# A finished batch's chain over 150 ticks instead of 126, its last steps one iteration later, with semaphores of their own and two other PSUM banks

## The chip, the core and the metric

The kernel runs on one core of one Trainium2 chip. The metric is the device time of one execution in microseconds (us). A core has five engines that run programs of their own and meet through semaphores: TensorE (PE; its weight loads are listed as PEld), VectorE (DVE), ScalarE (ACT), GpSimd (POOL) and SyncE (SP, which here only issues DMAs).

## What is computed

One perceiver block on 16 batches of 128 tokens with 512 numbers each. Cross attention to a context of 2048 rows (16 heads, one shared key and value head), then a linear attention with decay over chunks of 64 tokens (4 heads; a triangular system is solved for each), then a router that sends each token to one of 16 experts, of which each takes the first 128.

```
x = x + xattn(layernorm(x), ctx)            # softmax(Q K^T) V Wo + bo
x = x + retention(layernorm(x))             # (eye - A0)^-1 per chunk, then @ Wr
x = x + ffn(layernorm(x))                   # gate = softmax(x Wg), idx = argmax
    onehot = one_hot(idx); loc = sum((cumsum(onehot) - 1) * onehot)
    valid = loc < C
    dispatched[idx, loc] = x; h = relu(dispatched @ w1); y = h @ w2
```

## The kernel before

`attention` handles the 16 batches, `experts` the 16 experts after it. `attention` is a software pipeline with an order written out by hand. Every engine runs the same two loops, `for i in range(-1, B + 1)` over iterations and `for t in range(TICKS)` over 128 ticks. A tick is no time: it only sets in which order an engine's instructions stand. In iteration `i` three batches are in work:

- batch `i` is scored: in every second tick one of 64 score tiles (`score`, PE L370), its exponential `p` (ACT L553) and one sum of `p` into `psum` (`add_weights`, POOL L917, from the second tile of each of four groups on); eight tiles at a time go through `weigh` (the quads, PE L382). Ahead of a group 16 matmuls find its maxima (`largest`, PE L357, reduced on DVE L708 into `mpart`; two banks, so PE can be two ahead of DVE), and `turn_max` turns the result into the row `mrow`;
- batch `i + 1` is prepared (`prepare`: norm1, turned context tiles L332, queries L414, keys and values L437, `kvs` L743);
- batch `i - 1` is finished (`finish`). `sums` (PE L396, tick 9) adds up the weights and outputs; it waits for POOL's last sum of `p`. POOL's first sum of the next batch (tick 3) waits for `sums`, because it overwrites `psum`. Then come the reciprocals (DVE L764), `att` (L767, the tile `turned`), four projections `x1` (PE L336), `x1_add` with its statistics (DVE L771), norm2's root on POOL (L920, L922), `xn2`, six levels of the triangular solve (Y on DVE L794, XT on DVE L802, each with PE before and behind), `Vn`, `oT2`, four projections `x2`, `x2_add` (L809), norm3's root on POOL, `xn3` (DVE L814, into the tile `route`), `xn3T` (PE), the router's logits `lg` (PE L508), `eg` (ACT), the one-hot `oh` (DVE L823 to L830), `loc` (PE L513, L514), and the block under `row`: 13 small DVE instructions (L834 to L860), of which the second updates `before`, and the scatter of the rows on POOL (L962, L963).

The table `POST` and `LEVEL_AT` (L43 to L46) hold the tick of each step. An engine takes its steps strictly in this order, so a step that waits holds back all that stand behind it. PSUM has eight banks: two for maxima (`A_BANK`), two for scores (`B_BANK`), and one each of `PV_BANK`, `T_BANK`, `KV_BANK` and `P_BANK`; nearly all of `finish` goes through `P_BANK`. A semaphore counts the steps of one engine in the order of their names (`post_pe`, `post_act`, `post_dve`, `post_pool`). The last batch is finished in iteration 16, in which nothing else is left, over four banks.

Of the kernel before, what the change touches and what calls it, by code (L numbers as in the profile page):

```python
# [42 lines left out]
POST = dict(xb=2, sums=9, recip=[9, 10, 11, 12], att=13, x1=15, x1_add=18, norm2=19, xn2=22, ss=23, x12=24, rn=24,  # L43
            xn2T=25, rk=27, V=28, V_copy=31, rkT=34, I=38, XT1=40, X1=44, Vn=98, oT2=101, x2=104, x2_add=107,
            store=108, norm3=108, xn3=111, xn3T=115, lg=118, eg=119, oh=120, loc=123, row=125)
LEVEL_AT = [[47 + 9 * n, 50 + 9 * n, 53 + 9 * n] for n in range(LEVELS)]  # L46
# [55 lines left out]
def attention(nc, T, w1_first, w1_in):  # L102
    with ExitStack() as ctx:
# [90 lines left out]
        post_act = named("post_act", "ss0 ss1 ss2 ss3 xn2T rk0 rk1 rk2 rk3 V rkT X1 Vn oT2 xn3T eg")
        post_dve = named("post_dve", "x1 st2 mv2 xn2 XT1a MT IT x2 st3 mv3 xn3 lg0 lmax emax cand best oh "
                         "ohloc before loc valid locc row0 row d0 d1 sidx gate token token1")
        post_pool = named("post_pool", "xb ve2 rs2 x12 rm rn MT0 XT0 XT1 ve3 rs3")
# [1028 lines left out]
```

## Time and profile before

| | us |
|---|---|
| median of 3 runs | 2424.21 |
| lowest, highest | 2420.67, 2426.93 |
| profiled execution | 2427.98 |
| its span (first to last instruction) | 2426.1 |
| granted TensorE clock, mean | 0.946 |
| PE, POOL, DVE, ACT busy in the span | 2189.4, 1638.2, 1371.0, 1193.3 |

A page of the profile gives busy time by engine and the costliest groups. The timeline gives single instructions: start, duration, engine, line, operation, what it writes and reads, and in brackets how long the engine stood idle before it and who ended that. The granted clock is a share of full speed: 1.00 is 2.4 GHz, 0.50 is 1.2 GHz.

### The profile page before, as it was taken

Reading aid. Unit: us, or ns where it says so; the run is one execution under the profiler, and the core shown is the slowest. Engines: PE = TensorE matmul, PEld = TensorE weight load, DVE = VectorE, ACT = ScalarE, POOL = GpSimd, SP = SyncE. Lnnn points to the kernel's source line nnn. Section 1 sums busy time; section 2 is a strip of 40 time slices with the busy share of each in tenths; the row PEclk is TensorE's granted clock in tenths of the full one; section 3 lists DMA queues with packets and bytes.
Section 4 is the critical chain, followed back from the end, with each engine's and each line's share of the span. In section 5 each row is a group of like instructions: output and inputs, shape, how many; then the busy total and the mean of one; then the engine's idle time right before and its main releaser. Section 6 shows DMA issues by size and latency. Waiting matters only on the chain. (4 is left out here: it accounts for less than half of the span.)

```text
span 2426.1 us, 35019 instructions
## 1 busy us (share of the span) xinstructions
PE 2189.4 (90%) x12608; PEld 1429.9 (59%) x12608; DVE 1371.0 (57%) x2311; ACT 1193.3 (49%) x2237; POOL 1638.2 (68%) x1323
## 2 busy tenths in 40 slices
PE   5889898989998989898989898989898769999999
PEld 3435555546464646464646464645554448999998
DVE  2665757566667566666666666666665433333333
ACT  3555554646464646464645455555554313333333
POOL 0676878677777777777777777777777714655655
PEclk9889998999899989998999899989998889999999
DMA  4532120202020202121211111121120009999995
GB/s 160 188 113 66 40 82 24 83 23 83 23 83 23 83 26 80 40 66 40 66 47 58 51 59 63 43 66 42 59 79 9 18 14 375 350 363 346 362 363 189
DMA packets 108157, 263.75 MB, mean 109 GB/s; under 512 B 9849, under 2 KB 35065, under 8 KB 99792
## 3 DMA queue, kind: packets, MB, share of 16 engines
q1 hardware_dynamic: 98448, 235.32, 27.7%
q10 hardware_dynamic: 5952, 14.29, 1.6%
q0 software_dynamic: 3584, 11.90, 1.2%
q8 instruction: 101, 1.65, 0.3%
q14 instruction: 72, 0.59, 0.1%
HBM read 223.74 MB, written 25.72 MB: 103 GB/s over the span
## 5 line engine op out<-in xcount | busy, mean ns | idle before, releaser
L917 POOL TENSOR_TENSOR psum<-psum,p 128x512 f32<-128x512 f32 x896 | 1162.9, 1298 | 291.7 <-ACT p L553 197.7
L708 DVE TENSOR_REDUCE mpart<-bank 128x1 f32<-128x512 f32 x1024 | 675.0, 682 | 403.5 <-PE bank L357 396.1
L553 ACT ACTIVATE p<-bank 128x512 f32<-128x512 f32 x1024 | 596.8, 600 | 553.5 <-PE bank L370 543.6
L357 PE MATMUL bank<-kT,qT 96*128 96x512 f32 x1024 | 484.1, 480 | 62.6 <-DVE mpart L708 32.5
L370 PE MATMUL bank<-qT,kT 97*128 97x512 f32 x1024 | 502.4, 492 | 4.7 <-ACT p L553 4.0
L357 PEld LDWEIGHTS bank<-kT,qT 96*128 96x128 f32 x1024 | 199.6, 196 | 211.5 <-DVE mpart L708 104.6
L370 PEld LDWEIGHTS bank<-qT,kT 97*128 97x128 f32 x1024 | 201.7, 197 | 142.6 <-issue 113.6
L382 PE MATMUL bank<-p,v 128*32 128x512 f32 x2048 | 271.4, 651 | 0.0
L1159 POOL TENSOR_TENSOR w2l<-w,w2h 128x1024 fp32r<-128x1024 f32 x64 | 203.2, 3177 | 75.1 <-PE ebank L1074 54.4
L332 PE MATMUL bank<-cst,w_first 128*128 128x128 f32 x1024 | 164.1, 287 | 21.7 <-DMA w_first<-in_ctx 18.0
L332 PEld LDWEIGHTS bank<-cst,w_first 128*128 128x128 f32 x1024 | 134.3, 149 | 64.9 <-issue 29.4
L917 POOL TENSOR_TENSOR psum<-p 128x512 f32<-128x512 f32 x64 | 81.8, 1278 | 122.5 <-ACT p L553 101.6
L582 ACT COPY w_first<-bank 128x512 f32<-128x512 f32 x256 | 149.3, 586 | 15.0 <-PE bank L332 14.9
L1102 ACT ACTIVATE hh<-ebank 128x512 fp32r<-128x512 f32 x64 | 38.3, 599 | 225.3 <-PE ebank L1058 225.3
L1096 ACT CAST w2h<-w 128x2048 fp32r<-128x2048 f32 x64 | 121.5, 1898 | 44.1 <-DMA w<-in_w 44.1
L382 PEld LDWEIGHTS bank<-p,v 128*32 128x32 f32 x2048 | 56.7, 116 | 141.7 <-issue 107.3
L437 PE MATMUL bank<-w_first,wkv 128*64 128x512 f32 x512 | 125.7, 612 | 10.0 <-ACT w_first L582 9.8
L336 PE MATMUL bank<-wo,turned 128*128 128x512 f32 x128 | 90.3, 799 | 38.8 <-DVE turned L767 38.8
L1058 PE MATMUL ebank<-dT,w_first 128*128 128x128 f32 x1024 | 120.9, 279 | 0.9 <-DVE dT L1117 0.9
L1058 PEld LDWEIGHTS ebank<-dT,w_first 128*128 128x128 f32 x1024 | 120.0, 195 | 2.4 <-issue 1.2
L1123 DVE TENSOR_TENSOR w2l<-w,w2h 128x1024 fp32r<-128x1024 f32 x64 | 79.1, 1236 | 71.9 <-PE ebank L1074 48.0
L1128 DVE SCALAR_TENSOR_TENSOR hl<-ebank,hh 128x512 fp32r<-128x512 f32 x64 | 44.2, 691 | 133.4 <-ACT hh L1102 133.4
(159 smaller groups left out, 3137.8 us busy)
## 6 DMA issues: line engine op xcount, KB each, us to landing
w<-in_w SPq DMA_DIRECT2D x48, 2048.0 KB, 20.1
w_first<-in_ctx SPq DMA_DIRECT2D x64, 1024.0 KB, 4.9
w_first<-in_w SPq DMA_DIRECT2D x16, 2048.0 KB, 11.6
dispatched<-route ACTq DMA_DIRECT2D x17, 513.0 KB, 4.4
dis<-dispatched SPq DMA_DIRECT2D x16, 513.0 KB, 3.5
qT<-qh SPq DMA_DIRECT2D x128, 64.0 KB, 2.0
xin<-in_x SPq DMA_DIRECT2D x16, 256.0 KB, 2.6
qT<-qs SPq DMA_DIRECT2D x64, 64.0 KB, 2.0
```

The source lines that it names most:

```text
L332: ins = e.transpose(out[0:m, j * P:(j + 1) * P], src(j), ident)
L357: e.matmul(a[:], qT[b % 2][0:3 * HD, (4 * g + h) * P:(4 * g + h + 1) * P], kT[b % 2][0:3 * HD, c * 512:(c + 1) * 512], start=True, stop=Tr ...
L370: e.matmul(B_BANK[u % 2][:], kT[b % 2][0:3 * HD + 1, k * P:(k + 1) * P], qT[b % 2][0:3 * HD + 1, g * 512:(g + 1) * 512], start=True, stop= ...
L382: ins = e.matmul(PV_BANK[HD * j:HD * (j + 1), :], v1[b % 2][:, k + j, :], p[(UNITS * b + u + j) % NP][:], start=k == 0, stop=k == KB - 4)
L437: ins = e.matmul(KV_BANK[rows, :], wkv[:, j, :], cxT[c % 2][:, j, :], start=j < 2, stop=j >= 2)
L553: e.activation(p[n % NP][:], B_BANK[u % 2][:], ACT.Exp).then_inc(p_act.sem, 1)
L582: e.copy(cxT[c % 2][:, :, kk * P:(kk + 1) * P], turn_bank(b, ("t", k))[:].rearrange("p (c t) -> p c t", c=DC)).then_inc(cxT_act.sem, 1)
L708: e.tensor_reduce(mpart[g % 2][:, n:n + 1], A_BANK[(17 * g + n) % 2][:], AX.X, ALU.max).then_inc(max_dve.sem, 1)
L917: e.tensor_tensor(acc[:], first[:], p[(UNITS * b + u) % NP][:], ALU.add).then_inc(psum_pool.sem, 1)
L1058: ins = e.matmul(H_BANK[g][:, f * P:(f + 1) * P], w1[q][:, c, (4 * g + f) * P:(4 * g + f + 1) * P], dT[q][:, c, :], start=c == 0, stop=c = ...
L1096: e.copy(w2h[g][:], w2[q][:, 4 * g:4 * g + 4, :]).then_inc(w2h_act.sem, 1)
L1159: e.tensor_tensor(w2l[g % 2][:, 2:4, :], w2[q][:, 4 * g + 2:4 * g + 4, :], w2h[g][:, 2:4, :].bitcast(F32), ALU.subtract).then_inc(w2l_pool ...
```

## The change

The 126 ticks of `finish` become 150. Up to `X1` nearly every step moves one to three ticks later (`sums` to `att` stay at 9 to 13, `xb` goes from 2 to 12), a level takes 12 ticks instead of 9, and everything from `Vn` on goes later by 21 to 24 ticks: `Vn` from 98 to 119, `x2_add` from 107 to 130, which is tick 2 of the second next iteration. So the steps from there on are issued in iteration `i` for batch `i - 2`, ahead of the finish of batch `i - 1` in the same tick, and the loops get a 17th iteration of 22 ticks.

```diff
-POST = dict(xb=2, ... att=13, x1=15, x1_add=18, norm2=19, xn2=22, ... X1=44, Vn=98, oT2=101, x2=104, x2_add=107,
-            store=108, norm3=108, xn3=111, xn3T=115, lg=118, eg=119, oh=120, loc=123, row=125)
-LEVEL_AT = [[47 + 9 * n, 50 + 9 * n, 53 + 9 * n] for n in range(LEVELS)]
+POST = dict(xb=12, ... att=13, x1=16, x1_add=20, norm2=22, xn2=24, ... X1=47, Vn=119, oT2=123, x2=126, x2_add=130,
+            store=131, norm3=132, xn3=134, xn3T=138, lg=141, eg=142, oh=143, loc=147, row=149)
+LEVEL_AT = [[51 + 12 * n, 55 + 12 * n, 59 + 12 * n] for n in range(LEVELS)]
+TAIL = POST["row"] + 1 - TICKS
...
-        post_pe = named("post_pe", "x1 xn2T V rkT I X1 Vn oT2 x2 xn3T lg loc")
+        post_pe = named("post_pe", "x1 xn2T V rkT I X1")
+        late_pe = named("late_pe", "Vn oT2 x2 xn3T lg loc")
...
-            for i in range(-1, B + 1):
-                for t in range(TICKS):
+            for i in range(-1, B + 2):
+                for t in range(TICKS if i <= B else TAIL):
...
-                    if i >= 1:
+                    if i >= 2:
+                        finish(i - 2, t + TICKS)
+                    if 1 <= i <= B:
                         finish(i - 1, t)
```

The same split into `post_` and `late_` semaphores is made on ACT, DVE and POOL. The other change is in the banks: `sums` writes the weights' total into `PV_BANK` instead of `KV_BANK`, and `xn3T`, `lg` and `loc` use `KV_BANK` instead of `P_BANK`, with `V` instead of `turned` between them.

```diff
                 if k == 0 and (b or g):
-                    e.wait_ge(*(oS_act.at(b, g - 1) if g else oS_act.at(b - 1, HG - 1)))
+                    e.wait_ge(*(oS_act.at(b, g - 1) if g else o_dve.at(b - 1, "recip3")))
...
                 if b:
-                    e.wait_ge(*post_dve.at(b - 1, "before"))
-                if b + 1 < B:
-                    e.wait_ge(*kvs_dve.at(b + 1, 3))
-                for out, lhs, src in ((KV_BANK, cst[:, C_ONES, 0:HD], psum), (P_BANK, cst[:, C_STACK, 0:HD], oS)):
+                    e.wait_ge(*late_dve.at(b - 1, "x2"))
+                for out, lhs, src in ((PV_BANK, cst[:, C_ONES, 0:HD], psum), (P_BANK, cst[:, C_STACK, 0:HD], oS)):
...
                     elif b:
-                        e.wait_ge(*(o_dve.at(b - 2, "recip3") if b > 1 else kvs_dve.at(0, 3)))
+                        e.wait_ge(*(late_dve.at(b - 3, "before") if b > 2 else kvs_dve.at(b - 1, 3)))
...
                 if t == POST["xn3T"]:
-                    e.wait_ge(*post_dve.at(b, "xn3"))
-                    transposes(P_BANK, lambda h: cut(xn3, h)).then_inc(post_pe.sem, 1)
+                    e.wait_ge(*late_dve.at(b, "xn3"))
+                    if b + 2 < B:
+                        e.wait_ge(*kvs_dve.at(b + 2, 3))
+                    transposes(KV_BANK, lambda h: cut(xn3, h)).then_inc(late_pe.sem, 1)
```

POOL's program at the start of an iteration in the middle of the run, before (`psum` is a sum of p, `rs` a step of a root, `xr<-xr,bo` is xb):

```order
L917 TENSOR_TENSOR psum<-psum,p 128x512 [waits psum_pool,p_act]
L920 TENSOR_TENSOR rs<-mv,eps 128x1 [waits norm_dve]
L922 TENSOR_TENSOR rs<-rs,mhalf 128x1 [waits norm_pool]
L935 TENSOR_TENSOR xr<-xr,bo 128x512 [waits xr_in]
L917 TENSOR_TENSOR psum<-p 128x512 [waits sums_pe,p_act]
L917 TENSOR_TENSOR psum<-psum,p 128x512 [waits psum_pool,p_act] x8
```

and the same place after the change:

```order
L932 TENSOR_TENSOR rs<-mv,eps 128x1 [waits norm_dve]
L934 TENSOR_TENSOR rs<-rs,mhalf 128x1 [waits norm_pool]
L929 TENSOR_TENSOR psum<-p 128x512 [waits sums_pe,p_act]
L932 TENSOR_TENSOR rs<-mv,eps 128x1 [waits late_dve]
L934 TENSOR_TENSOR rs<-rs,mhalf 128x1 [waits late_pool]
L929 TENSOR_TENSOR psum<-psum,p 128x512 [waits psum_pool,p_act] x4
L947 TENSOR_TENSOR xr<-xr,bo 128x512 [waits xr_in]
L929 TENSOR_TENSOR psum<-psum,p 128x512 [waits psum_pool,p_act] x5
L974 TENSOR_TENSOR pad_pool<-mhalf 128x1 [waits late_dve]
L975 DMA dispatched<-route,sidx 2176x1026
L932 TENSOR_TENSOR rs<-mv,eps 128x1 [waits post_dve]
L934 TENSOR_TENSOR rs<-rs,mhalf 128x1 [waits post_pool]
```

The pair that waits for `late_dve` is norm3's root of the older batch; it has come to stand behind the sum that waits for `sums_pe`. The scatter has come to stand ahead of norm2's root, the pair that waits for `post_dve`.

DVE's program from norm1's last step (`xin<-xin,mv,rs`) to att (`turned<-bank,x`), before:

```order
L727 TENSOR_SCALAR xin<-xin,mv,rs 128x512 [waits norm_pool]
L708 TENSOR_REDUCE mpart<-bank 128x1 [waits a_pe] x3
L764 RECIPROCAL x<-bank 128x128 [waits sums_pe] x2
L708 TENSOR_REDUCE mpart<-bank 128x1 [waits a_pe]
L764 RECIPROCAL x<-bank 128x128 [waits sums_pe] x2
L708 TENSOR_REDUCE mpart<-bank 128x1 [waits a_pe]
L767 TENSOR_TENSOR turned<-bank,x 128x512 [waits o_dve]
```

and after:

```order
L737 TENSOR_SCALAR xin<-xin,mv,rs 128x512 [waits norm_pool]
L718 TENSOR_REDUCE mpart<-bank 128x1 [waits a_pe]
L824 TENSOR_SCALAR route<-route,mv,rs 128x512 [waits late_pool]
L718 TENSOR_REDUCE mpart<-bank 128x1 [waits a_pe] x2
L774 RECIPROCAL x<-bank 128x128 [waits sums_pe] x2
L718 TENSOR_REDUCE mpart<-bank 128x1 [waits a_pe]
L774 RECIPROCAL x<-bank 128x128 [waits sums_pe] x2
L718 TENSOR_REDUCE mpart<-bank 128x1 [waits a_pe]
L828 COPY lg<-bank 128x16 [waits late_pe]
L830 TENSOR_REDUCE sc<-lg 128x1 [waits late_dve]
L777 TENSOR_TENSOR turned<-bank,x 128x512 [waits o_dve]
```

xn3 (`route<-route,mv,rs`) now stands ahead of the reciprocals, with two of the three maxima behind it, and lg's two steps stand ahead of att.

## Rows read from the trace of the kernel before

**Rows 1.** The page: busy time by engine; the costliest group (busy, mean ns, idle).

```profile
PE 2189.4 (90%) x12608; PEld 1429.9 (59%) x12608; DVE 1371.0 (57%) x2311; ACT 1193.3 (49%) x2237; POOL 1638.2 (68%) x1323
L917 POOL TENSOR_TENSOR psum<-psum,p 128x512 f32<-128x512 f32 x896 | 1162.9, 1298 | 291.7 <-ACT p L553 197.7
```

**Rows 2.** L396's matmuls (start of first and last); then stretches with busy time, clock.

```profile
L396 PEld LDWEIGHTS bank<-psum,cst x128: 106/109/155, 174.4 to 1929.4; 128*32 128x32 f32 x128
...
core 0: us, PE busy (x) PEld busy (x) DVE busy (x) ACT busy (x) POOL busy (x), PEclk, DMA share, GB/s
404.30:437.50 33.20, 28.59 (x131) 13.31 (x131) 22.03 (x46) 14.63 (x34) 24.57 (x26) 0.83 0.07 25
482.10:521.60 39.50, 36.47 (x210) 22.66 (x208) 28.02 (x48) 21.40 (x43) 30.72 (x27) 0.99 0.05 17
398.30:401.70 3.40, 1.79 (x9) 0.96 (x8) 2.50 (x8) 1.70 (x6) 2.97 (x3) 1.00 0.00 1
401.70:408.50 6.80, 6.80 (x26) 3.13 (x26) 5.62 (x18) 1.79 (x3) 5.79 (x6) 0.50 0.14 40
```

**Rows 3.** Timeline of PE, ticks 0 to 28 of one batch: start, duration, instruction.

```profile
404.37 0.63 PE L370 MATMUL bank<-qT,kT 97*128 97x512 f32 x1
...
413.56 0.50 PE L357 MATMUL bank<-kT,qT 96*128 96x512 f32 x1
...
419.87 2.08 PE L336 MATMUL bank<-wo,turned 128*128 128x512 f32 x2 [2.31 <-DVE turned L767]
...
428.47 1.02 PE L336 MATMUL bank<-wo,turned 128*128 128x512 f32 x2
...
436.19 0.50 PE L357 MATMUL bank<-kT,qT 96*128 96x512 f32 x1 [1.24 <-ACT mrow L559]
...
437.34 0.48 PE L370 MATMUL bank<-qT,kT 97*128 97x512 f32 x1
```

**Rows 4.** PE late in the batch (timeline), and PE's waits from 400 to 1860.

```profile
505.99 1.04 PE L336 MATMUL bank<-wr,turned 128*128 128x512 f32 x2
...
507.09 1.02 PE L336 MATMUL bank<-wr,turned 128*128 128x512 f32 x2
...
514.46 0.66 PE L332 MATMUL bank<-cst,route 128*128 128x128 f32 x4
...
515.79 1.07 PE L508 MATMUL bank<-wg,turned 128*128 128x16 f32 x8
...
519.86 0.40 PE L513 MATMUL bank<-oh,cst 128*128 128x16 f32 x2 [0.98 <-DVE oh L830]
...
PE bank L488 <- DVE xr L802: 7.8, 24, 0.5
PE bank L340 <- DVE Y L794: 6.3, 24, 0.3
```

**Rows 5.** Timeline of POOL at the start of a batch, and of PE in batch 1.

```profile
407.61 0.20 POOL L962 TENSOR_TENSOR pad_pool<-mhalf 128x1 f32<-128x1 f32 x1 [0.40 <-DVE route L858]
407.98 1.11 POOL L963 DMA_INDIRECT dispatched<-route,sidx  x1 [0.17 <-issue]
...
410.37 0.19 POOL L920 TENSOR_TENSOR rs<-mv,eps 128x1 f32<-128x1 f32 x1
410.63 0.57 POOL L922 TENSOR_TENSOR rs<-rs,mhalf 128x1 f32<-128x1 f32 x1
...
413.81 1.28 POOL L917 TENSOR_TENSOR psum<-p 128x512 f32<-128x512 f32 x1 [1.34 <-PE bank L396]
...
174.36 1.94 PE L396 MATMUL bank<-psum,cst 128*32 128x512 f32 x8 [6.52 <-POOL psum L917]
```

**Rows 6.** Timeline of DVE: xn3, the block's start, a reciprocal pair, xn2 of the last batch.

```profile
394.83 1.33 DVE L814 TENSOR_SCALAR route<-route,mv,rs 128x512 f32<-128x512 f32 x1
...
404.36 0.16 DVE L834 TENSOR_TENSOR oh<-bank,oh 128x16 f32<-128x16 f32 x1
...
414.70 1.76 DVE L764 RECIPROCAL x<-bank 128x128 f32<-128x128 f32 x2
...
1945.44 0.55 DVE L776 TENSOR_SCALAR xn<-x,mv,rs 128x512 f32<-128x512 f32 x1 [0.95 <-POOL rs L922]
```

More of the change, by code:

```diff
@@ L42 @@
 LOAD_AT = [t + 6 for t in TILE_AT[3::4]]
[L43 to L46 removed]
+POST = dict(xb=12, sums=9, recip=[9, 10, 11, 12], att=13, x1=16, x1_add=20, norm2=22, xn2=24, ss=25, x12=26, rn=27,
+            xn2T=28, rk=30, V=31, V_copy=35, rkT=36, I=39, XT1=43, X1=47, Vn=119, oT2=123, x2=126, x2_add=130,
+            store=131, norm3=132, xn3=134, xn3T=138, lg=141, eg=142, oh=143, loc=147, row=149)
+LEVEL_AT = [[51 + 12 * n, 55 + 12 * n, 59 + 12 * n] for n in range(LEVELS)]
+TAIL = POST["row"] + 1 - TICKS
 MAX_AT, MAX_TURN = [15 * n // 8 - 39 for n in range(KB)], -8
@@ L190, in attention @@
         o_dve = named("o_dve", "recip0 recip1 recip2 recip3 att")
-        post_pe = named("post_pe", "x1 xn2T V rkT I X1 Vn oT2 x2 xn3T lg loc")
[L194 to L197, printed above, removed]
+        post_pe = named("post_pe", "x1 xn2T V rkT I X1")
+        post_act = named("post_act", "ss0 ss1 ss2 ss3 xn2T rk0 rk1 rk2 rk3 V rkT X1")
+        post_dve = named("post_dve", "x1 st2 mv2 xn2 XT1a MT IT")
+        post_pool = named("post_pool", "xb ve2 rs2 x12 rm rn MT0 XT0 XT1")
+        late_pe = named("late_pe", "Vn oT2 x2 xn3T lg loc")
+        late_act = named("late_act", "Vn oT2 xn3T eg")
+        late_dve = named("late_dve", "x2 st3 mv3 xn3 lg0 lmax emax cand best oh ohloc before loc valid locc row0 row "
+                         "d0 d1 sidx gate token token1")
+        late_pool = named("late_pool", "ve3 rs3")
         y_pe, z_pe, xt_pe = count("y_pe", LEVELS), count("z_pe", LEVELS), count("xt_pe", LEVELS - 1)
@@ L521, in _ @@
                     e.wait_ge(*dec_dve.at(DEC_DVE - 1))
-                for t in range(TICKS):
+                for t in range(TICKS if i <= B else TAIL):
                     if 0 <= i < B and t % 2 == 0:
@@ L528, in _ @@
                         weigh(b, u)
-                    if i >= 1 and t == POST["sums"]:
+                    if 1 <= i <= B and t == POST["sums"]:
                         sums(i - 1)
@@ L674, in once @@
                         dec_act.sem, 1)
-            for i in range(-1, B + 1):
-                for t in range(TICKS):
+            for i in range(-1, B + 2):
+                for t in range(TICKS if i <= B else TAIL):
                     if 0 <= i < B and t % 2 == 0:
@@ L830, in finish @@
[L830 to L840 removed]
+                        late_dve.sem, 1)
@@ L862, in once @@
+                    e.tensor_copy(route[:, 2 * D + 1:ROUTE].bitcast(U32), token[:]).then_inc(late_dve.sem, 1)
+                    e.wait_ge(*late_dve.at(b, "token"))
+                    e.tensor_scalar(token[:], token[:], float(P), None, ALU.add).then_inc(late_dve.sem, 1)
             def once(t):
@@ L965, in finish @@
                         in_=route[:], in_offset=None).then_inc(scat_out.sem, 16)
-            for i in range(-1, B + 1):
+            for i in range(-1, B + 2):
                 if i == 1:
@@ L970, in _ @@
                     e.wait_ge(*zeroed.at(ZEROES - 1))
-                for t in range(TICKS):
+                for t in range(TICKS if i <= B else TAIL):
                     if 0 <= i < B and t % 2:
```

166 lines of the change are left out of this document (84 added, 82 removed).

## The prediction

> **What bounds the kernel now.** I read the page first: PE is busy 90% of the span, and the other engines 49 to 68% [rows 1]. The sums of all 16 batches start between 174.4 and 1929.4 us, so 15 stretches take 117.0 us each [rows 2]; the experts behind them are not touched. So I looked at what PE does inside one of them, by its own timeline. The reader is to see there where PE stands still and on whom it waits. In the batch whose tick 0 is the score at 404.37, tick 28 is reached at 437.34 [rows 3]: 28 ticks of 128 take 33.0 us, more than twice their share. In that piece PE waits 2.31 us for att (L767) before x1 and 1.24 us for the row of maxima [rows 3]. At the end of a batch it waits 0.98 us for the one-hot before loc [rows 4].
>
> Then the clock. From 398.3 to 401.7 PE is busy 1.79 of 3.4 us, and in the 6.8 us behind it the granted clock is 0.50, the lower level of 1.2 GHz [rows 2]. So some 1.6 us of waiting in such a stretch cost more than their own length. POOL matters although it has time left: its 960 sums of p take about 1.30 us each [rows 1], in program order, and the first of a batch waits for sums [rows 5]. That order decides what follows.
>
> **What leaves ticks 28 to 128.** Two of four x2 projections stand 1.10 us apart with a 0.24 us maximum between them, so one is 0.86 and two are 1.7; xn3T lasts 0.66, lg 1.07, one part of loc 0.40 [rows 4], and modelled ends overlap the next start by a quarter of a us, so they are 0.4, 0.9 and 0.5. Together 3.5. The one-hot wait goes: 1.0 (four ticks instead of three). The level waits (Y and XT) are 6.3 and 7.8 us over the 12.4 batches of the window, 1.1 a batch [rows 4]; with a level each 12 ticks I count them as gone. The low clock of the batch's end reaches 2.7 us back of tick 0 in this batch and none in the next; half of it lost, on average 0.7. Some 0.2 of small waits. Sum: **6.5 us less** a batch, where PE alone limits.
>
> **What the first 28 ticks get.** (a) The POOL step of norm3 (tick 132, which is tick 4 of the next iteration) now stands behind the first sum of p (tick 3), and that one waits for PE's sums. Before, the same step stood at tick 108, and only norm1's and xb ahead of that wait. So the chain now is: sums issued at 413.56, that sum of p 413.81 to about 415.05, the two steps of the root 0.8 (410.37 to 411.20), xn3 on DVE 1.33, PE's xn3T at about 417.4 [rows 3, 5, 6]. PE comes there after 1.0 us: it **waits 2.9 us** where it did not wait. DVE, too, stands at xn3 with the reciprocals behind it; lg and its maximum add 0.4 ahead of att. Two maxima that it did before them follow xn3 as well. The first reciprocal moves from 414.70 to about 418.5, and x1 from 419.87 to about 424.1 [rows 3, 6]: **4.2 us more**. xn3T and lg lie in this wait and cost nothing of their own. (b) Two x2 projections beside the quads of tick 1, and x2_add on DVE ahead of the maxima: the low clock that went there (a full 4 us of 6.8) pays for them. 0.2 more. (c) From x1 to tick 28: loc 0.5 for a turn that moves ahead of x1 (0.4); the block of small steps under `row`, 404.36 to 407.61, where POOL is let go, now stands between x1_add and kvs [rows 5, 6]. PE's kv waits for `before` in it, 1.2 us, and in exchange the wait for the maxima's row (1.24) goes, because ss comes after it on ACT. But norm2's root on POOL now stands behind the scatter, which waits for the whole block: x1_add 1.0 us after the start of the last projection (that one's 1.02 us [rows 3]), its statistics, a maximum and the small reduction behind it 2.6, the block 3.3, the scatter 1.5 (407.61 to 409.09), the root 0.8, xn2 1.3, the next maximum 0.7. So PE's maximum of tick 28 can start about 11.0 us after that projection, and PE is there at about 10.1. 0.9 more. The clock: two waits of nearly 3 us instead of one, so the slow stretch may cover all of x1; taken at 1.0, with 0 and 2.3 as bounds. Sum of (c): 2.1. Together **6.5 us more**.
>
> A rule of the Trainium skill speaks to (a): SBUF — State Buffer, section "Who interferes with whom", says that a DVE tensor_scalar in its two-port mode and a POOL instruction exclude each other for the whole instruction. The trace agrees: the form took 1.33 us with POOL summing and 0.55 us with POOL idle [rows 6]. By the rule the worst xn3 would be 1.28 + 0.55 = 1.83, which makes the sum 0.5 us a batch larger, 7 us in all.
>
> **The sum.** Thirteen batches (finishing in iterations 2 to 14): -6.5 + 6.5 = 0. Iteration 1 has no late steps of an older batch: -6 to 0, taken -6. Iteration 15 prepares nothing, and POOL's 60 sums of 1.30 us are most of it: 0. Behind the last sums everything is a chain: lg's two DVE steps 0.4, loc at the lower clock twice 0.5, the block and the scatter before norm2 3.3 and 1.5: **+6.2**. Total +0.2 on an execution of 2427.98 us, which is 0.16% above the median of 2424.21. Forecast **2424 us**.
>
> **Rivals.** *Faster: the clock holds.* If the two waits do not pull the clock down, the part from x1 to its last projection (419.87 to 428.47, 8.6 us [rows 3]) costs about 6.1, and the 1.0 of (c) is not paid: -3.5 a batch, 13 times, 2379 us; if it holds in every second batch, 2401. For it: batches alternate already. Against: 1.6 us without work were enough at 398.3 [rows 2].
>
> [...]
>
> *Slower: the crowd on DVE and POOL.* Between ticks 0 and 28 DVE has 22.0 of 33.2 us of work [rows 2]; it gets xn3 (1.3), x2_add with its statistics (1.6), lg and the one-hot (2.5) and keeps the block (3.3), which moves to the other side of x1_add, and PE may run only two maxima ahead of it. If each of the four places where another engine waits for it (xn3, att, one-hot, kvs) is late by 0.5 to 0.7 us more than worked out, it is +2.5 a batch: 2457. It decides from the point where DVE has no idle time left between the sums and kvs. For it: the reciprocals move later by 4 us into what idle time there is. Against: 11 us of it are there now.
>
> *POOL takes the gain.* Ticks 72 to 128 take 39.5 us and POOL works 30.7 of them [rows 2]. After the change PE needs about 35, and POOL's 27 sums need 35 too. In the first batch, where PE had nothing to finish, PE ran ahead and then stood 6.52 us at sums waiting for POOL [rows 5]. If 1.0 of the 6.5 comes back there: +13, 2437.
>
> **How the numbers follow.** Forecast case, the sum to within 1 us a batch (2411 to 2437): 0.42, of it 0.15 faster, 0.18 same, 0.09 slower. Clock holds in part or in full (2375 to 2411): 0.20, faster. The crowd (2437 to 2475): 0.26, slower. POOL: 0.12, of it 0.06 same, 0.06 slower. A measurement of this kernel tells 0.3% (7 us) from no change. That gives faster 0.35, same 0.24, slower 0.41. The range 2388 to 2460 leaves out half of the clock's case and a quarter of the crowd's, under 0.2. The forecast case alone is 2411 to 2437.
>
> **What would show it.** Right: a wait of 2.5 to 3 us before xn3T ended by DVE's xn3, POOL's root right behind the first sum of p; x1 some 10.5 us after the sums instead of 6.3; no wait before loc, full clock around tick 0, no level waits; tick 28 at 39 us, ticks 28 to 128 in 77 to 78. Wrong: xn3T without a wait would mean that norm3's step got ahead of the sums, and the change would be 50 us faster. A wait at sums for POOL of over 1 us is the third rival; waits before maxima (mpart) of over 2 us a batch are the second.

## The result and the profile after

| | before | after |
|---|---|---|
| median, us | 2423.12 (6 runs) | 2440.51 (6 runs) |
| lowest to highest | 2420.67 to 2426.93 | 2436.0 to 2445.49 |
| profiled execution, its span | 2427.98, 2426.1 | 2442.13, 2440.3 |
| mean granted clock | 0.946 | 0.953 |

The ratio after to before is 1.007, with a 95% interval of 1.0053 to 1.0087. The change is slower by 0.7%, small but clear of the 0.3% (7 us) that the prediction took for the least difference that can be told.

The page of after, busy time by engine, for [rows 1]:

```profile
PE 2171.8 (89%) x12608; PEld 1431.0 (59%) x12608; DVE 1351.8 (55%) x2311; ACT 1189.3 (49%) x2237; POOL 1626.9 (67%) x1323
```

The sums of all batches (start of the first and the last), for the first line of [rows 2]:

```profile
L400 PEld LDWEIGHTS bank<-psum,cst x128: 106/109/155, 172.7 to 1940.1; 128*32 128x32 f32 x128
```

PE's first instruction of the experts in the timeline, after and then before:

```profile
2019.32 1.08 PE L1061 MATMUL ebank<-eident,dis 128*128 128x128 f32 x4 [11.67 <-DMA dis<-dispatched]
```

```profile
2005.22 1.08 PE L1047 MATMUL ebank<-eident,dis 128*128 128x128 f32 x4 [11.24 <-DMA dis<-dispatched]
```

The experts begin 14.1 us later, and that is the whole difference of the two spans (14.2). By the starts of each batch's first score and of `sums`, it is made up so: 2.5 less before iteration 1, 5.5 less in iteration 1, 15.5 more in iterations 2 to 14, 3.2 more in iteration 15 up to the last `sums`, 3.4 more from there to the experts. The 2.5 is no effect of the change: nothing is finished before iteration 1, and in the twelve kernels below that have the new order this point falls anywhere between 158.4 and 166.2 us (before: 162.4).

So the loss is made in the steady batches, some 1.3 us in each. This table cuts an average batch (batches 2 to 13) at instructions of PE; each number is a mean over twelve batches of one profiled execution:

| us per batch | before | after |
|---|---|---|
| tick 0 to sums | 7.92 | 8.60 |
| sums to x1 | 8.16 | 12.23 |
| x1 to tick 28 | 16.97 | 16.67 |
| ticks 28 to 128 | 84.68 | 81.58 |
| whole batch | 117.7 | 119.1 |
| of it, PE waits (each over 0.1) | 9.3 | 11.6 |
| of it, time at granted clock 0.50 | 10.2 | 8.8 |

One batch of after in PE's timeline, from tick 0 (the score at 636.56) to tick 28 (the score at 673.78), for [rows 3]:

```profile
636.56 0.80 PE L376 MATMUL bank<-qT,kT 97*128 97x512 f32 x1
...
644.72 0.50 PE L363 MATMUL bank<-kT,qT 96*128 96x512 f32 x1 [0.95 <-DVE mpart L718]
...
647.01 0.50 PE L363 MATMUL bank<-kT,qT 96*128 96x512 f32 x1
...
650.87 1.12 PE L338 MATMUL bank<-cst,route 128*128 128x128 f32 x4 [2.69 <-DVE route L824]
...
657.38 1.92 PE L342 MATMUL bank<-wo,turned 128*128 128x512 f32 x2 [1.13 <-DVE turned L777]
...
668.79 1.94 PE L441 MATMUL bank<-w_first,wkv 128*64 128x512 f32 x8 [1.73 <-DVE sc L847]
...
673.78 0.48 PE L376 MATMUL bank<-qT,kT 97*128 97x512 f32 x1
```

The new waits are xn3T (2.69, behind xn3 on DVE) and `kv`, the matmuls of keys and values (1.73, behind the step that updates `before`; the trace names the step next to it). The releaser of the first, in the timelines of POOL and DVE, for [rows 5, 6]; and the block under `row` with the scatter behind it:

```profile
647.26 1.27 POOL L929 TENSOR_TENSOR psum<-p 128x512 f32<-128x512 f32 x1 [5.31 <-PE bank L400]
648.49 0.19 POOL L932 TENSOR_TENSOR rs<-mv,eps 128x1 f32<-128x1 f32 x1
648.76 0.55 POOL L934 TENSOR_TENSOR rs<-rs,mhalf 128x1 f32<-128x1 f32 x1
...
670.11 0.20 POOL L974 TENSOR_TENSOR pad_pool<-mhalf 128x1 f32<-128x1 f32 x1 [1.98 <-DVE route L868]
```

```profile
649.34 1.48 DVE L824 TENSOR_SCALAR route<-route,mv,rs 128x512 f32<-128x512 f32 x1 [3.62 <-POOL rs L934]
...
668.39 0.17 DVE L844 TENSOR_TENSOR oh<-bank,oh 128x16 f32<-128x16 f32 x1
...
670.06 0.15 DVE L870 TENSOR_SCALAR token<-token 128x1 f32<-128x1 f32 x1
```

POOL stood 5.31 us at the first sum of p, did that, and only then the root; DVE stood 3.62 us at xn3 for it. The block, for which [rows 5, 6] gave 3.3 us, took 1.8 (668.39 to 670.2), while POOL stood idle. It takes 1.8 in every batch of after; in the steady batches of before it took 3.4 to 3.6 and 4.3 in turn.

PE's waits from 400 to 1860, after, for [rows 4] (total, times, longest):

```profile
PE bank L363 <- DVE mpart L718: 48.6, 63, 1.4
PE bank L338 <- DVE route L824: 35.4, 13, 3.1
PE bank L441 <- DVE sc L847: 21.4, 12, 2.1
...
PE bank L342 <- DVE turned L777: 10.7, 11, 1.9
```

and the same stretch of before, of those that [rows 4] did not hold:

```profile
PE bank L336 <- DVE turned L767: 30.0, 13, 2.3
...
PE bank L357 <- DVE mpart L708: 22.4, 37, 1.5
PE bank L513 <- DVE oh L830: 12.9, 13, 1.0
```

The one-hot wait and the XT waits are gone, the att wait has shrunk from 30.0 to 10.7, and the waits for a maximum (`mpart`) have doubled.

### The profile page after: what moved, and what is told of

It reads as the page before. It is cut to its first block and busy times, and to the rows that moved or that the text cites. A ratio compares the mean times of both kernels' runs of the same rounds, so it can differ in the third digit from the quotient of the medians.

```text
span 2440.3 us, 35019 instructions
## 1 busy us (share of the span) xinstructions
PE 2171.8 (89%) x12608; PEld 1431.0 (59%) x12608; DVE 1351.8 (55%) x2311; ACT 1189.3 (49%) x2237; POOL 1626.9 (67%) x1323
## 5 line engine op out<-in xcount | busy, mean ns | idle before, releaser
L929 POOL TENSOR_TENSOR psum<-psum,p 128x512 f32<-128x512 f32 x896 | 1148.5, 1282 | 319.0 <-ACT p L561 227.4
L363 PE MATMUL bank<-kT,qT 96*128 96x512 f32 x1024 | 469.0, 467 | 92.2 <-DVE mpart L718 66.5
L376 PE MATMUL bank<-qT,kT 97*128 97x512 f32 x1024 | 495.8, 486 | 4.6 <-ACT p L561 3.5
L388 PE MATMUL bank<-p,v 128*32 128x512 f32 x2048 | 265.4, 639 | 0.0
L1072 PEld LDWEIGHTS ebank<-dT,w 128*128 128x128 f32 x1024 | 117.5, 192 | 1.4
L1072 PE MATMUL ebank<-dT,w 128*128 128x128 f32 x1024 | 118.2, 275 | 0.0
## 6 DMA issues: line engine op xcount, KB each, us to landing
w_first<-in_w SPq DMA_DIRECT2D x16, 2048.0 KB, 11.6
```

What stands on the lines that cost most here:

```text
L363: e.matmul(a[:], qT[b % 2][0:3 * HD, (4 * g + h) * P:(4 * g + h + 1) * P], kT[b % 2][0:3 * HD, c * 512:(c + 1) * 512], start=True, stop=Tr ...
L376: e.matmul(B_BANK[u % 2][:], kT[b % 2][0:3 * HD + 1, k * P:(k + 1) * P], qT[b % 2][0:3 * HD + 1, g * 512:(g + 1) * 512], start=True, stop= ...
L388: ins = e.matmul(PV_BANK[HD * j:HD * (j + 1), :], v1[b % 2][:, k + j, :], p[(UNITS * b + u + j) % NP][:], start=k == 0, stop=k == KB - 4)
L929: e.tensor_tensor(acc[:], first[:], p[(UNITS * b + u) % NP][:], ALU.add).then_inc(psum_pool.sem, 1)
L1072: ins = e.matmul(H_BANK[g][:, f * P:(f + 1) * P], w1[q][:, c, (4 * g + f) * P:(4 * g + f + 1) * P], dT[q][:, c, :], start=c == 0, stop=c = ...
```

## The experiments

All runs are compared with the kernel before on the same chip, where its median was 2423.9 to 2425.8 us. "Waits" and "low clock" are those of the table above, per batch. They come from one profiled execution of each kernel, and the times in us are medians of 4 to 12 executions.

### Is it the root of norm3 behind the first sum of p?

My theory was the wait of step (a): the root stands behind a sum that waits for `sums`. The rivals were that the crowd on DVE, or the moved work itself, made the first 28 ticks long.

**The root first** (e1_root_first): it moves from tick 4 to tick 2 of the next iteration, ahead of that sum.

```diff
-            store=131, norm3=132, xn3=134, ...
+            store=131, norm3=130, xn3=134, ...
```

> Edit on the changed kernel: norm3's root on POOL at tick 130 instead of 132, so that it stands ahead of the first sum of p that waits for PE's sums; nothing else. Theory A (POOL's order is what the first 28 ticks cost): PE's wait of 2.69 us before xn3T falls under 0.5, DVE's wait of 3.62 us at xn3 under 1, x1 starts 6.5 to 7 us after the sums instead of 10.4, ticks 0 to 28 take 33.5 to 34.5 us instead of 37.2; with 14 such batches 2385 to 2400 us. Rival B (DVE is simply crowded): the wait comes back at att or before maxima, ticks 0 to 28 stay above 36 us, 2425 us or more.

Measured: 2377.39 us, ratio 0.9797 [0.9784, 0.981]. That is 63 us under the changed kernel. POOL, PE and DVE at the same place of a batch:

```profile
634.31 0.19 POOL L932 TENSOR_TENSOR rs<-mv,eps 128x1 f32<-128x1 f32 x1 [2.17 <-DVE mv L714]
634.58 0.72 POOL L934 TENSOR_TENSOR rs<-rs,mhalf 128x1 f32<-128x1 f32 x1
637.39 1.28 POOL L929 TENSOR_TENSOR psum<-p 128x512 f32<-128x512 f32 x1 [2.09 <-PE bank L400]
```

```profile
637.72 0.60 PE L338 MATMUL bank<-cst,xin 128*128 128x128 f32 x4
638.16 0.60 PE L338 MATMUL bank<-cst,route 128*128 128x128 f32 x4
```

```profile
635.78 0.54 DVE L824 TENSOR_SCALAR route<-route,mv,rs 128x512 f32<-128x512 f32 x1
```

The root now stands in front of the sum, xn3 runs while POOL is idle (0.54 instead of 1.48 us) and xn3T follows the instruction before it without a wait. The batch shrinks by 5.0 us, from 119.1 to 114.0. Only 2.0 of that are waits (11.6 to 9.6): xn3T's 2.69 is gone, and att's went from 0.90 to 1.75. The other 3.0 are the clock: time at 0.50 fell from 8.8 to 2.8 us a batch, and half of 6.0 is 3.0 (an estimate: at half the clock half of the time counts as lost). The expectation named the mechanism but not this part, so the time came out under its 2385 to 2400. Of the 63 us between the two spans 60 lie in batches 2 to 13. The same stretch in both kernels, after first, then the experiment (the clock is the third number from the end):

```profile
580.00:900.00 320.00, 289.72 (x1660) 175.80 (x1653) 203.28 (x348) 170.96 (x343) 236.11 (x205) 0.97 0.16 49
```

```profile
580.00:900.00 320.00, 293.31 (x1729) 178.66 (x1728) 211.32 (x372) 179.96 (x369) 248.82 (x219) 1.00 0.18 57
```

**The root one sum later** (e9_root_later): the same edit the other way, norm3 at 133, behind two sums of p.

```diff
-            store=131, norm3=132, xn3=134, ...
+            store=131, norm3=133, xn3=134, ...
```

> Edit on the changed kernel: norm3's root at tick 133 instead of 132, one more sum of p (1.28 us) ahead of it on POOL; the cost in question made larger. Theory A (POOL's order sets PE's wait before xn3T): that wait grows from 2.69 to 3.9 to 4.0 us, x1 starts 1.2 us later, 14 batches: 2455 to 2462 us. Rival B (DVE's crowd sets it): less than 0.5 us more a batch, under 2448 us.

Measured: 2473.23 us, ratio 1.0196 [1.0179, 1.0213]. PE's wait for xn3 over 400 to 1860:

```profile
PE bank L338 <- DVE route L824: 49.2, 12, 4.1
```

The wait went from 2.69 to 4.1, as the length of one sum says, and the whole batch from 119.1 to 120.8, with 1.3 more waits and low clock up from 8.8 to 10.2, which is another 0.7. Over the twelve batches that is 21 us. The medians are 33 apart and the spans 31, more than I had expected. Of the other 10, iteration 14 has 4.7 (its low clock went from 6.8 to 17.1 us), iteration 15 has 2.9, the stretch behind the last sums 1.7, and what is left lies at the start. With three positions (130, 132, 133: 2377, 2441, 2473) and the wait following each, the theory stands.

### Are the banks and semaphores to blame?

**Only they** (e4_banks_only): the changed kernel with the old `POST` and `LEVEL_AT`, `TAIL = 0`, and the store in its old place.

```diff
-POST = dict(xb=12, ... norm3=132, ... row=149)
-LEVEL_AT = [[51 + 12 * n, 55 + 12 * n, 59 + 12 * n] for n in range(LEVELS)]
-TAIL = POST["row"] + 1 - TICKS
+POST = dict(xb=2, ... norm3=108, ... row=125)
+LEVEL_AT = [[47 + 9 * n, 50 + 9 * n, 53 + 9 * n] for n in range(LEVELS)]
+TAIL = 0
```

> The changed kernel's banks and semaphores with the old ticks (POST, LEVEL_AT and the store's tick as in the kernel before), so one part of the change alone. Theory A (the banks and waits are free): within 3 us of the kernel before, 2420 to 2427 us, the same waits in the first 28 ticks. Rival B (the banks matter: quads of the next batch now wait for the reciprocals, or sums for other steps): slower by 5 us or more with a wait at the quads of tick 17.

Measured: 2425.73 us, ratio 1.0005 [0.9995, 1.0014], with the batch cut as before to a tenth of a us in every row of the table. With the old ticks, banks and semaphores cost nothing, as predicted, so the loss comes with the new table of ticks. It does not follow that the banks are free under the new ticks. The wait of the keys' matmuls for `before` exists only because `loc` now uses `KV_BANK` (the wait on `late_dve` in the second diff of "The change"), and with the new ticks PE stood there 1.79 us a batch. The new ticks with the old banks were not run.

### The block under row

**Split** (e2_block_late): its first two instructions (through `before`) stay at 149, the other 11 and the scatter go to 156, behind norm2's root.

```diff
-            ... loc=147, row=149)
+            ... loc=147, row=149, row2=156)
-TAIL = POST["row"] + 1 - TICKS
+TAIL = POST["row2"] + 1 - TICKS
...
                     e.tensor_tensor(before[:], before[:], oh[:], ALU.add).then_inc(late_dve.sem, 1)
+                if t == POST["row2"]:
```

> Edit on the changed kernel: of the block of 13 small DVE steps the first two stay at tick 149, the other 11 and the scatter move to tick 156, behind norm2, xn2 and the norm of the keys on POOL and DVE. Theory A: norm2's root no longer stands behind the scatter, xn2 comes 2 to 3 us earlier after x1, and 0.5 to 1 us a batch comes back: 2425 to 2434 us. The wait of 2.69 us before xn3T stays. Rival B (the block cost nothing where it stood, since POOL was idle there and it took 1.8 us): within 3 us of 2440, or slower by what it does to the maxima at ticks 28 to 32.

Measured: 2434.25 us, ratio 1.0039 [1.0027, 1.0052]. The average batch is the same within 0.2 us (118.9). Between the two profiled executions the span fell by 9.6 us: 2.2 in batches 2 to 13, 3.9 in iteration 15, 3.4 behind the last sums. The last of these is PE's wait for xn2 there, after the changed kernel first, then this one (stretch 1930 to 2020):

```profile
PE bank L338 <- DVE xn L786: 6.3, 1, 6.3
```

```profile
PE bank L338 <- DVE xn L786: 3.2, 1, 3.2
```

So the scatter in front of norm2's root costs 3.1 us once, in the tail, and in the steady batches next to nothing; my (c) had charged it there. In iteration 15 PE's waits for maxima fell from 7.5 to 3.9 us (before: 2.5) and its low clock from 26.3 to 22.3, so the block's place matters in that iteration too. How, I did not follow.

**Both** (e3_both), e1 and e2 together.

> Both edits of the two runs before together on the changed kernel. Theory A (two waits in a row, each with its own price): the gains add up, 2375 to 2392 us. Rival B (one hides the other): no better than the root's edit alone.

Measured: 2369.58 us, ratio 0.9773 [0.9759, 0.9787]. Against e1 it gives 7.8 us, about what e2 gave alone (6.3). The profiled execution (2375.59) lies 6 us above the median; it has 4.3 us of low clock a batch, so e3's row in the tables is somewhat too high.

**Before updated ahead of x1_add** (e7_before_ahead): e3 with the first two steps of the block at 148. That is tick 20, the tick of x1_add, and the older batch goes first, so they stand ahead of it instead of behind it.

```diff
-            ... loc=147, row=149, row2=156)
+            ... loc=147, row=148, row2=156)
```

> On the run with both edits: row at 148 instead of 149, so that DVE updates before ahead of x1_add (tick 20) and not behind its statistics; the other 11 steps stay at 156. Theory A (PE's wait of 1.79 us before the keys' matmul is the new wait on before that the bank swap brought, and only its place on DVE makes it long): that wait falls under 0.5, ticks 0 to 28 take 30.3 to 31 us instead of 31.8, 2350 to 2358 us. Rival B (the wait moves on to kvs or the queries): 2366 us or more.

Measured: 2353.41 us, ratio 0.9701 [0.9685, 0.9717]. PE's waits over 400 to 1860 have no line for `before` any more, where the changed kernel had 21.4 us in twelve waits; the two largest are now:

```profile
PE bank L363 <- DVE mpart L718: 50.5, 66, 1.4
PE bank L342 <- DVE turned L777: 25.4, 14, 2.4
```

That is what the first theory expected (2350 to 2358). A batch takes 112.7; against e3 (114.8) waits fell by 1.4 and low clock from 4.3 to 2.6, which is 0.9 more.

### Why did ticks 28 to 128 give back only 3.1 us?

The waits in them did not fall by 2.3 as predicted but rose from 4.06 to 4.74. By tick (mean us a batch): before, 0.62 for a maximum at tick 42, 0.46 for `w_first` at 46, 1.2 for Y and XT of the levels, 1.61 for `mrow` and the one-hot at 122; after, for a maximum 0.92 at tick 42, 0.90 at 46, 0.66 at 74 and 0.44 at 106, and for `mrow` 0.25 to 0.48 at 58, 90 and 122. Is it the spacing of the levels, or single steps of DVE that stand in front of a maximum?

**The old spacing** (e5_spacing9):

```diff
-LEVEL_AT = [[51 + 12 * n, 55 + 12 * n, 59 + 12 * n] for n in range(LEVELS)]
+LEVEL_AT = [[51 + 9 * n, 54 + 9 * n, 57 + 9 * n] for n in range(LEVELS)]
```

> Edit on the changed kernel: a level of the triangular solve takes 9 ticks again (LEVEL_AT starts at 51, steps of 9 instead of 12), Vn and all behind it stay. It measures the spread by itself. Theory A (the spread takes the waits for Y and XT out, which the prediction priced at 1.1 us a batch): these waits return, 28 to 128 takes 82 to 82.5 us instead of 81.2, 2450 to 2458 us. Rival B (the waits before maxima, 3.06 us a batch where the kernel before had 0.62, come from the spread, levels now falling beside other work of DVE): they fall by 1 us or more and the time is 2440 or less.

Measured: 2475.28 us, ratio 1.0193 [1.0176, 1.021], slower than the first theory's 2450 to 2458. Its waits in ticks 28 to 128 are 4.83 against 4.74, so nearly the same sum: those for a maximum fell (in total 37.6), and the level waits came back.

```profile
PE bank L363 <- DVE mpart L718: 37.6, 60, 1.0
...
PE bank L492 <- DVE xr L812: 6.4, 24, 0.3
```

What it lost was the clock: 13.7 us a batch at 0.50 instead of 8.8, which is 2.4 of the 2.8 us by which its batch is longer (the profiled execution, 2484.94, lies 10 us above the median, with a mean clock of 0.939 where the others had 0.947 to 0.950, so this is its upper end). The clock fell at tick 46 in seven of the twelve batches, where the changed kernel had that in two. Nothing in its rows says why it fell there oftener; that stays open.

**The products earlier** (e6_products_earlier): e3 with `rkT` and `I` one tick earlier.

```diff
-            ... rkT=36, I=39, XT1=43, ...
+            ... rkT=35, I=38, XT1=43, ...
```

> On the run with both edits (root first, block late; 2369.6 us): rkT at 35 and I at 38 instead of 36 and 39, so that DVE's three products stand at ticks 38 to 40 as in the kernel before and not at 39 to 41 around kvs at 40. Theory A (the two waits of 0.92 and 0.94 us before maxima near tick 41 and 46 are this crowd): they fall to about 0.6 in all, 28 to 128 from 81.2 to about 80, 2353 to 2360 us. Rival B (they come from PE's three maxima close together there): unchanged, 2366 to 2373 us.

Measured: 2392.25 us, ratio 0.9862 [0.9846, 0.9879], 23 us slower than e3 and outside of both theories. The wait for a maximum at tick 42 fell from 0.92 to 0.62 and the one at 46 is gone, but 0.87 for XT1 and 0.68 for V came in their place (waits in ticks 28 to 128: 5.39 against 4.65). Over 400 to 1860:

```profile
PE bank L338 <- POOL xr L968: 11.7, 13, 1.9
PE bank L338 <- ACT V L631: 8.8, 13, 0.7
```

In the profiled executions it is 15 us behind (2390.67 against 2375.59), and batches 2 to 13 make 7.5 of them (115.4 against 114.8). Iteration 14 makes 4.7: it had 10.2 us of low clock and e3 none. Iteration 15 makes 2.4 and iteration 1 another 1.4. The other 8 us between the medians are in no trace, since e3's was taken 6 us above its median.

**The products later** (e10_products_later), on top of e7: `kvs` and two maxima stand ahead of the products on DVE.

```diff
-            ... I=39, XT1=43, X1=47, ...
+            ... I=41, XT1=44, X1=47, ...
```

> The fastest kernel so far (norm3's root ahead of the first sum of p, before ahead of x1_add, the block late; 2353.4 us) with one more edit: I at tick 41 instead of 39 and XT1 at 44 instead of 43, so that on DVE the step kvs and two maxima stand ahead of the three products instead of between and behind them. In the changed kernel PE waits 0.92 us a batch at tick 42 and 0.90 at tick 46 for a maximum on DVE (mpart). Theory one, the waits come from this crowd (products that wait for PE's I with kvs and the maxima queued behind): the two waits fall from 1.86 us to under 0.6 a batch, ticks 28 to 128 take about 80 us instead of 81.2, and the time is 12 to 18 us lower, 2335 to 2342. Theory two, the waits only change place, as they did when the products came earlier: the waits of ticks 28 to 128 stay at 4.3 to 5 us, the XT step on POOL or a level is waited for instead, and the time is 2350 to 2365.

Measured: 2350.99 us, ratio 0.9687 [0.9666, 0.9707]. The wait at tick 42 is gone (0.92 to under 0.15), the one for a maximum at 46 stays (0.94), and beside it `w_first` goes from 0.19 to 0.56 and 0.31 for a product is new. The sum falls from 4.77 to 4.38 and ticks 28 to 128 from 81.69 to 80.75; the clock takes most back ahead of tick 28, with 3.4 us at 0.50 in each batch instead of 2.6 on average. Between my two theories: half a gain, half a change of place. The medians of e7 and e10 are 2.4 us apart and their intervals overlap, so the gain itself is not clear of noise.

**The levels one tick earlier** (e11_levels_shifted), on e7:

```diff
-LEVEL_AT = [[51 + 12 * n, 55 + 12 * n, 59 + 12 * n] for n in range(LEVELS)]
+LEVEL_AT = [[50 + 12 * n, 54 + 12 * n, 58 + 12 * n] for n in range(LEVELS)]
-            ... XT1=43, X1=47, ...
+            ... XT1=43, X1=46, ...
```

> The fastest kernel so far (2353.4 us) with every step of the six levels one tick earlier (50, 54, 58, then every 12) and X1 at 46. If the waits for a maximum at ticks 74 and 106 (0.66 and 0.44 us a batch) come from level steps of DVE that wait for PE with maxima behind them, another phase moves or removes them: 0.3 to 1.0 us a batch less, 2338 to 2349. If the spread alone sets the waits, nothing changes: 2350 to 2357.

Measured: 2357.05 us, ratio 0.9732 [0.9697, 0.9767], 3.6 us over e7 with intervals that overlap. The maxima's waits moved (0.66 at 74 to 0.17, 0.44 at 106 gone, 0.79 new at 78) and a wait for POOL's XT1 at tick 46 came, because X1 follows it sooner:

```profile
PE bank L363 <- DVE mpart L718: 36.4, 51, 1.4
...
PE bank L338 <- POOL xr L968: 17.7, 13, 1.6
```

The sum fell from 4.77 to 4.16, yet the time did not: low clock went from 2.6 to 4.6 us a batch, and 113.3 is longer than e7's 112.7.

So these waits hang on which steps of DVE stand in front of a maximum. Four other placements moved them and changed their sum by -0.6 to +0.7 us, and none came near the 1.8 that the forecast needed (4.06 less 2.3). For the maxima at ticks 42, 74 and 106 this is shown by e10 and e11, in which those waits moved or went with the steps. The one at tick 46 (0.94) stayed as it was in e10, and in e6 and e11 another wait took its place, so its cause is not shown. Which placement would remove them all is open.

### Two small ones and the best version

**lg behind att** (e12_lg_behind_att), on e7: on DVE, lg's two steps stand behind att.

```diff
-            ... lg=141, eg=142, oh=143, ...
+            ... lg=142, eg=143, oh=144, ...
```

> The fastest kernel so far (2353.4 us) with lg, eg and oh one tick later, so that on DVE the two steps of lg stand behind att instead of ahead of it. PE waits 1.75 us a batch for att before x1. If lg's two steps (0.16 to 0.25 us each) are what makes att late, the wait falls by 0.3 to 0.5 us, 2346 to 2350. If att is late by the reciprocals alone, the two steps are nothing on this path and the time stays at 2353 within 4 us; if the one-hot becomes late for loc, it is 3 to 8 us slower.

Measured: 2348.49 us, ratio 0.968 [0.966, 0.97]. PE's wait for att fell from 1.75 to 1.49 a batch, sums to x1 from 8.45 to 8.16, as expected, and the time fell by 4.9. But the average batch fell only from 112.7 to 112.6, since its low clock rose from 2.6 to 3.1, so the twelve batches explain 1.2 us; the rest lies before and behind them, and the intervals of e7 and e12 just overlap.

**e10 and e12 together** (e13_both_small):

> The fastest kernel so far with both of the small edits that gained: I at 41 and XT1 at 44, and lg, eg, oh one tick later. Alone they gave 2.4 and 4.9 us. If what each gains stands in its own place (ticks 40 to 46, and before x1), they add: 2345 to 2348, ticks 28 to 128 in 80.6 and sums to x1 in 8.2. If the granted clock takes a gain back, as it did in the first of them (3.4 us of lower clock in every batch instead of in every second), they do not add: 2348 to 2354.

Measured: **2341.19 us, ratio 0.965 [0.9634, 0.9666]**, the fastest of all, 3.5% under the kernel before. Its edit is the two diffs above. It gained 12.2 over e7, where the parts gave 2.4 and 4.9 alone, so more than both and more than either case of the expectation. Waits are 7.6 a batch (e7 8.2), the sum of the two savings; low clock is 2.8, where the parts alone had 3.4 and 3.1 (e7 2.6). So in these executions the clock took most of the gain from each alone, and less from both. Batches 2 to 13 make 8.1 of the 9.9 us between the profiled executions of e7 and e13. Why the clock fell less often with both is open.

## Why the prediction was wrong

The forecast was 2424 as no change, and the time is 2440.5: inside the range of 2388 to 2460, but past the end of the forecast's own 2411 to 2437, on the slower side. The chance for slower (0.41) was the largest of the three; the forecast case was not the one that came.

**The failed step is the 6.5 us that leave ticks 28 to 128.** They were 3.1 (84.68 to 81.58). By its terms:
- moved work 3.5: right, about 3.6. The 3.1 is these 3.6 and 0.15 less lost to the clock, minus 0.7 more waits. PE's busy time at full clock says nearly the same: 76.17 us in the batch of after below, and 80.08 in the batch of before (its stretch first).

```profile
437.30:521.60 84.30, 80.08 (x483) 50.96 (x481) 53.67 (x87) 49.86 (x98) 62.43 (x52) 1.00 0.21 66
```

```profile
673.80:754.90 81.10, 76.17 (x466) 48.63 (x465) 51.81 (x79) 50.27 (x103) 64.19 (x53) 1.00 0.21 66
```

- one-hot, level and small waits 2.3: these did go (2.4), but 3.1 others came, 2.4 of them for maxima. I had counted which waits end and not what PE, which then comes sooner, meets next. The text had the sign for it ("waits before maxima of over 2 us a batch" for the second rival): they were 3.06 in these ticks and 4.1 in all.
- low clock 0.7: low time went from 1.4 to 1.1 us there, which is 0.15.

**The first 28 ticks** got 4.4 instead of 6.5:
- (a), predicted 4.2 more to x1: right in path and size. PE's wait for xn3 was 2.69 (predicted 2.9), sums to x1 grew by 4.07, and from the maximum behind sums to x1 it is 10.4 us (647.01 to 657.38; predicted 10.5). e1 and e9 show the cause.
- (b), predicted 0.2: 0.7. The low clock that had been there did go (3.7 to 0 us, worth 1.9) and paid for most of the moved work (2.2 more); waits rose by 0.3, to 0.95 us for a maximum at tick 8 in every batch.
- (c), predicted 2.1: it came out at 0.3 less than nothing. The wait for `before` was underestimated (1.79, predicted 1.2) and `mrow` kept 0.46 of its 1.24. But the 0.9 of tick 28 did not come, since the block took 1.8 us and not 3.3 with POOL idle beside it, and the 1.0 of clock did not either: from x1 to tick 28 low time fell from 4.6 to 3.8 (worth 0.4). Waits there rose by 0.75, and PE's work fell by 0.66, in part because x1 stands one tick later, so that this piece is a tick shorter.

So the gain was put 3.4 too high and the cost 2.1 too high, and the difference is the 1.3 a batch that the kernel lost. Both errors have one kind: a term taken from the rows of before (a wait that ends, a step beside a working POOL) and not from what stands beside it after the change.

Three of the prediction's readings are off without moving its sum by much. 33.0 us for 28 ticks are 1.3 times their share of 117.0, and not more than twice. The steps from x1's last projection to the maximum of tick 28 add up to 11.2 us and not 11.0. The terms of (c) add up to 2.0 and not 2.1.

**Iteration 1** was right (5.5 less, predicted 6; 2.8 to 8.3 less in the other kernels with the new order). **Iteration 15**, taken at 0, cost 3.2: PE waited 5.4 us instead of 2.7 for POOL at the last sums and 7.5 instead of 2.5 for maxima, with 4.0 us less low clock. In e2 the 5.3 at the sums stayed, the maxima's went down to 3.9, and the iteration took 0.8 less than before; which points to the maxima more than to POOL. **The tail**, predicted 6.2, cost 3.4, of which e2 shows 3.1 to be the scatter in front of norm2's root.

**The rivals.** *The clock holds*: it did not (8.8 us a batch at 0.50). In e1, without xn3T's wait, it held through ticks 0 to 28 of all twelve batches; but e10, which has no such wait either, had a fall at tick 16 in eleven of them. *The crowd*: the nearest to what came. The time is between the forecast and its 2457. But none of the four places that it named (xn3, att, one-hot, kvs) made PE wait longer than worked out; the wait for `before` did, and so did the maxima, which wait in DVE's queue behind other steps. *POOL takes the gain*: no wait at sums in the steady batches; there is one in iteration 15 alone.

The sentence that the change would be 50 us faster if xn3T had no wait was right: e1 is 47 us under the kernel before.

## What the runs add up to

For all kernels, the same three numbers per batch (batches 2 to 13; "rest" is the batch less the waits less half of the low-clock time):

| kernel | batch | waits | low clock | rest |
|---|---|---|---|---|
| before | 117.7 | 9.3 | 10.2 | 103.4 |
| after | 119.1 | 11.6 | 8.8 | 103.1 |
| e4, banks only | 117.7 | 9.3 | 10.1 | 103.3 |
| e2, block late | 118.9 | 11.5 | 8.5 | 103.1 |
| e1, root first | 114.0 | 9.6 | 2.8 | 103.0 |
| e3, both | 114.8 | 9.6 | 4.3 | 103.1 |
| e9, root later | 120.8 | 12.8 | 10.2 | 102.8 |
| e5, spacing 9 | 121.8 | 10.7 | 13.7 | 104.3 |
| e6, products earlier | 115.4 | 10.3 | 3.7 | 103.2 |
| e7, before ahead | 112.7 | 8.2 | 2.6 | 103.2 |
| e10, products later | 112.6 | 7.8 | 3.4 | 103.1 |
| e11, levels shifted | 113.3 | 7.6 | 4.6 | 103.5 |
| e12, lg behind att | 112.6 | 7.9 | 3.1 | 103.1 |
| e13, best | 112.0 | 7.6 | 2.8 | 103.0 |

But for e5 (104.3, which I can't explain) the rest is 103.1 within 0.4. In these kernels a batch is 103 us of PE's work, whatever the order, plus waits, plus half of what runs at the lower level. What the tables of ticks changed is in the two middle columns.

## To carry to other kernels

When a step is moved in a pipeline with an order by hand, look on each engine for the first instruction in front of it that waits for something of the same iteration: two ticks too late (132 instead of 130) cost 63 us, and made of a gain of 47 a loss of 17. Removing a wait was worth its length only where PE met nothing else sooner, so ask for each removed wait what PE reaches next and whose queue that stands in. And keep a ledger of work, waits and low clock for a batch: here it closed to 0.4 us in all but one kernel, and showed that the clock could give or take as much as the waits.
